# A recommendation tower on one core: TensorE's order of turns, products and gram units in each tile of 128 rows

## Chip, cores and metric

The kernel runs on 1 core of one Trainium2 chip. The metric is the device time of one execution in microseconds (us); lower is better.

## What is computed

For each of 2048 rows the reference takes one row of 128 numbers from each of 27 tables, forms all 351 dot products of two different ones of these 27 vectors, and sends vectors, dot products and 16 further numbers through three layers.

```python
e = jnp.stack([tbl_0[ids[:, 0]], ..., tbl_26[ids[:, 26]]], axis=1)      # (2048, 27, 128)
gram = jnp.einsum('bfd,bgd->bfg', e, e)                                 # (2048, 27, 27)
h = concatenate([e.reshape(B, -1), gram[:, triu_i, triu_j], dense_ctx], axis=1)   # 3823 columns
h = jnp.maximum(h @ W_top1 + b_top1, 0.0)                               # 3823 x 512
h = jnp.maximum(h @ W_top2 + b_top2, 0.0)                               # 512 x 256
y = h @ W_top3                                                          # 256 x 1
```

## The kernel before

The batch is cut into 16 tiles (t = 0 to 15) of 128 rows. The 27 features of a tile lie in seven groups (g = 0 to 6) of four, the last of three. Each engine has its whole program written out by hand in its own order, and the engines meet only at semaphores. Tiles 0 to 14 have one loop body each on TensorE, ScalarE and VectorE; tile 15 has an order of its own, which the change leaves as it is.

What happens to a tile, by engine:

- GpSimd gathers the rows of the tables into `emb`, one indirect DMA for each feature (L242). There is one `emb` for all tiles: before it gathers group g of tile t+1 it waits on `s_pe_t` until TensorE has turned group g of tile t (L236). It works strictly in the order of the groups.
- TensorE turns a group (`turn_group`, L263: four transposes at L269 into one of two banks of `ps_t`, then one increment of `s_pe_t`). It waits for the gather of the group (`s_gather`) and for the group two back to have left its bank (`s_emb_lo`, L267).
- ScalarE copies the turned group from `ps_t` into the high part of `emb_x` (`split_group`, L528, the copy is L534), VectorE subtracts to get the low part (L645) and raises `s_emb_lo`. Turn, copy and subtraction together make the group ready.
- TensorE multiplies each feature by its weights (`multiply`, L289: three matmuls of 128x512, L298 to L300, into `ps_acc`, called "one product" here). The first product of a group waits for `s_emb_lo`.
- The gram stage: 16 units of two matmuls (`gram_unit`, L308, the matmul is L323) into three banks of `ps_gram`. Unit 0 waits until the last group is ready (L310). Unit n waits until unit n-3 has been copied out. ScalarE copies out the even units (L582, four copies each), VectorE the odd ones (L666).
- VectorE turns, adds and packs the dot products of tile t-1 into `cols` during the products of tile t (L680 to L706).
- The columns' product of tile t-1 is part of tile t: TensorE turns `cols` (`turn_columns`, L359, L352), ScalarE copies it (`take_columns`, L546), TensorE adds it to the sum of tile t-1 (`multiply_columns`, L376, L356) and raises `s_acc`. ScalarE applies the relu (`relu_h1`, L561), TensorE turns h1 (`turn_h1`, L390, L393), ScalarE copies it (`take_h1`, L567), and after the gram stage TensorE makes layer 2 (`layer_2`, L397, L400). VectorE ends it (`layer_3`).

ScalarE takes its instructions in order: a copy that waits holds all that stand behind it. So in tile t the order on ScalarE is: groups 0 to 3, `take_columns`, group 4, `relu_h1`, group 5, `take_h1`, group 6, then the even units.

TensorE's order in a tile 1 to 14 before: products of group 0, turn of group 2, products of group 1, turn 3, products of group 2, `turn_columns`, turn 4, `multiply_columns`, products of group 3, turn 5, `turn_h1`, two products, turn 6, two products (`BEFORE_UNIT[0]`), gram units 0 to 15 with one or two products ahead of some, and with the turns of groups 0 and 1 of the next tile behind units 8 and 14, then `layer_2` and the products that are left.

Of the kernel before, what the change touches and what calls it, by code (L numbers as in the profile page):

```python
# [5 lines left out]
def dlrm_tower_kernel(nc, dense_ctx, ids, tables, w_top1, b_top1, w_top2, b_top2, w_top3, out):  # L6
# [7 lines left out]
    BATCH, NF = ids.shape  # L14
# [10 lines left out]
    GF = 4  # L25
    GROUPS = [list(range(f, min(f + GF, NF))) for f in range(0, NF, GF)]
    NG = len(GROUPS)
# [18 lines left out]
    UNITS = Q // QB  # L46
# [8 lines left out]
    with ctx:  # L55
# [84 lines left out]
        def emb_part(part, f):  # L140
            return emb_x[:, part, :, f]
# [4 lines left out]
        def turned_bank(n, g):  # L146
            return ps_t[:, n % 2, 0:GF * P].rearrange("p (b f) -> p b f", f=GF)[:, :, 0:len(GROUPS[g])]
# [114 lines left out]
        def _(pe):  # L262
            def turn_group(t, g):  # L263
                n = NG * t + g
                pe.wait_ge(s_gather[g], (t + 1) * 16 * len(GROUPS[g]))
                if n >= 2:
                    pe.wait_ge(s_emb_lo, n - 1)  # L267
                for i, f in enumerate(GROUPS[g]):
                    last = pe.transpose(turned_bank(n, g)[:, :, i], emb[:, f * D:(f + 1) * D],  # L269
                                        ident[:, :])  # L270
                last.then_inc(s_pe_t, 1)
# [17 lines left out]
            def multiply(t, f):  # L289
                g = f // GF  # L290
                if f == 0 and t >= 2:
                    pe.wait_ge(s_h1, t - 1)
                if f == GROUPS[g][0]:
                    pe.wait_ge(s_emb_lo, NG * t + g + 1)
                    if t == 0:
                        pe.wait_ge(s_w_lo, GROUPS[g][-1] + 1)
                acc = ps_acc[:, t % 2, :]
                pe.matmul(acc, emb_part(0, f), w_hi[:, f, :], start=(f == 0), stop=False)  # L298
                pe.matmul(acc, emb_part(0, f), w_lo[:, f, :], start=False, stop=False)  # L299
                last = pe.matmul(acc, emb_part(1, f), w_hi[:, f, :], start=False, stop=False)  # L300
                if f == GROUPS[g][-1]:
                    last.then_inc(s_emb_mm, 1)

            def multiply_group(t, g):
                for f in GROUPS[g]:
                    multiply(t, f)

            def gram_unit(t, k):  # L308
                if k == 0:
                    pe.wait_ge(s_emb_lo, NG * t + NG)  # L310
                    if t == 0:
                        pe.wait_ge(s_pads, 1)
                n = UNITS * t + k
                if n >= BANKS:

                    m = n - BANKS
                    if m % 2 == 0:
                        pe.wait_ge(s_act_raw, m // 2 + 1)
                    else:
                        pe.wait_ge(s_dve_raw, m // 2 + 1)  # L320
                for i in range(QB):
                    q = k * QB + i
                    last = pe.matmul(  # L323
                        ps_gram[:, n % BANKS, i * NJ * XW:(i + 1) * NJ * XW],
                        gram_weights(q), gram_stream(q), start=True, stop=True)
                last.then_inc(s_gram, 1)
# [32 lines left out]
            def turn_columns(t):  # L359
                pe.wait_ge(s_cols, t + 1)  # L360
                if t > 0:
                    pe.wait_ge(s_h2, t)
                if t == 0:
                    pe.wait_ge(s_ones, 2)
                for n in range(NCC):
                    last = turn_chunk(n, ps_late[:, n * P:(n + 1) * P])
                last.then_inc(s_cols_t, 1)
# [8 lines left out]
            def multiply_columns(t):  # L376
                pe.wait_ge(s_cols_out, t + 1)
                if t == 0:
                    pe.wait_ge(s_w_late, 64)
                for n in range(NCC):  # L380
                    last = multiply_chunk(t, n)
                last.then_inc(s_acc, 1)
# [7 lines left out]
            def turn_h1(t):  # L390
                pe.wait_ge(s_h1, t + 1)
                for k in range(K2):
                    last = pe.transpose(ps_late[:, k * P:(k + 1) * P], h1[:, k * P:(k + 1) * P],  # L393
                                        ident[:, :])
                last.then_inc(s_h1_t, 1)
# [42 lines left out]

            BEFORE_UNIT = [2, 0, 0, 2, 0, 0, 1, 0, 0, 1, 0, 0, 1, 0, 0, 0]
            assert len(BEFORE_UNIT) == UNITS and sum(BEFORE_UNIT) <= NF - 4 * GF

            pe.wait_ge(s_ident, 1)
            turn_group(0, 0)
            turn_group(0, 1)
            for t in range(TILES - 1):
                multiply_group(t, 0)  # L450
                turn_group(t, 2)
                multiply_group(t, 1)
                turn_group(t, 3)
                multiply_group(t, 2)
                if t > 0:
                    turn_columns(t - 1)
                turn_group(t, 4)
                if t > 0:
                    multiply_columns(t - 1)
                multiply_group(t, 3)  # L460
                turn_group(t, 5)
                if t > 0:
                    turn_h1(t - 1)
                f = 4 * GF
                for _ in range(GF if t == 0 else 2):
                    multiply(t, f)
                    f += 1
                turn_group(t, 6)
                for k in range(UNITS):
                    for _ in range(min(BEFORE_UNIT[k], NF - f)):  # L470
                        multiply(t, f)
                        f += 1
                    gram_unit(t, k)
                    if k in (8, 14):
                        turn_group(t + 1, (k - 8) // 6)
                if t > 0:
                    layer_2(t - 1)
                while f < NF:
                    multiply(t, f)
                    f += 1  # L480

            t = TILES - 1
            todo = list(range(NF))

            def multiply_next(count):
                for _ in range(count):
                    multiply(t, todo.pop(0))

            turn_group(t, 2)
            multiply_next(6)
            turn_group(t, 3)
            multiply_next(6)
# [27 lines left out]
        def _(act):  # L522
# [83 lines left out]
            for t in range(TILES - 1):  # L606
                for g in range(NG):
                    if t == 0:
                        for c in GROUPS[g]:
                            split_weights(c)  # L610
                    split_group(t, g)
                    if t > 0 and g == 3:
                        take_columns(t - 1)
                    if t > 0 and g == 4:
                        relu_h1(t - 1)
                    if t > 0 and g == 5:
                        take_h1(t - 1)
                for k in range(0, UNITS, 2):
                    take_blocks(t, k)
            t = TILES - 1  # L620
# [178 lines left out]
```

## Time and profile before

| what | value |
|---|---|
| median of 3 runs | 712.8 us (710.17 to 718.01) |
| the profiled execution, its own time | 709.83 us |
| span of the profiled execution, first to last instruction | 708.0 us |
| mean granted TensorE clock | 0.908 of full speed |
| TensorE matmuls busy | 574.9 us, 81% of the span |
| GpSimd busy | 416.2 us, 59% |
| VectorE busy | 347.6 us, 49% |
| ScalarE busy | 232.3 us, 33% |

Rows of the profile name an engine (PE TensorE's matmuls, PEld its weight loads, DVE VectorE, ACT ScalarE, POOL GpSimd), a source line (L298), what is written <- what is read, and for a stretch of instructions their number (x6). Times are microseconds from the start of the span. A number in square brackets is how long the engine stood idle just ahead of that instruction, and what released it; "remote" and "issue" say that the profile found no instruction that did. A row of stretches has from:to, its length, the busy time and count of PE, PEld, DVE, ACT and POOL, the granted TensorE clock as a share of full speed, the share of the DMA engines and GB/s.

### The profile page before, as it was taken

The numbers are of one execution on the slowest core, as the hardware profiler recorded it, in microseconds if no ns is written. First come the engines' busy times: TensorE is split into PE (matmuls) and PEld (weight loads), VectorE is DVE, ScalarE is ACT, GpSimd is POOL, SyncE is SP. The second block draws the span as 40 slices with busy tenths as digits, with TensorE's granted clock in tenths as the row PEclk, the third lists the DMA queues.
The fourth block names the chain that finished last, engine by engine and source line by source line (L and its number), as shares of the span: only waits on it lengthen the run. The fifth ranks groups of instructions, "written<-read, shape, count | busy, mean of one in ns | idle before, by whom it ended". The sixth has DMA issues, their size and how long they took to land.

```text
span 708.0 us, 7882 instructions
## 1 busy us (share of the span) xinstructions
PE 574.9 (81%) x2578; PEld 504.6 (71%) x2578; DVE 347.6 (49%) x1140; ACT 232.3 (33%) x703; POOL 416.2 (59%) x450
## 2 busy tenths in 40 slices
PE   2606688989889898959959896897968979698898
PEld 1505577868778787948848795786857868697786
DVE  4305462819264563808337281554707355372755
ACT  4204423324251513315232331514315161323441
POOL 6775565666666565665746667365664666556001
PEclk9956899989989998989989899799987999989999
DMA  6613411111111111111111111011110111111000
GB/s 211 217 52 110 131 45 44 46 46 44 45 45 50 41 49 41 48 45 39 47 29 50 44 42 52 27 49 42 46 52 26 49 41 49 42 41 46 12 1 1
DMA packets 19581, 37.84 MB, mean 53 GB/s; under 512 B 7780, under 2 KB 8804, under 8 KB 19540
## 3 DMA queue, kind: packets, MB, share of 16 engines
q0 software_dynamic: 13824, 28.34, 15.1%
q1 hardware_dynamic: 5716, 8.99, 4.0%
q8 instruction: 21, 0.34, 0.2%
q14 instruction: 20, 0.16, 0.1%
HBM read 37.30 MB, written 0.01 MB: 53 GB/s over the span
## 4 chain that ended last, share of the span: by engine, by line
PE 59%; another core or an unknown queue 20%; DVE 8%; issue 6%; ACT 5%; DMA 1%; SPq 0%; ACTq 0%; DVEq 0%
PE ps_acc L298 12%; PE ps_acc L299 11%; PE ps_acc L300 11%; PE ps_gram L323 10%; DVE g_buf L666 6%; PE ps_acc L356 6%; PE ps_t L269 5%; PE ps_gram L400 3%; ACT g_buf L582 2%; DVE emb_x L645 1%; DMA g_buf<-in_W_top 1%; ACT emb_x L534 1%; ACT h_t L571 1%; PE ps_gram L352 1%
## 5 line engine op out<-in xcount | busy, mean ns | idle before, releaser
L242 POOL DMA_INDIRECT emb<-in_tbl,idx x405 | 385.8, 953 | 233.4 <-issue 109.4
L298 PE MATMUL ps_acc<-w_hi,emb_x 128*128 128x512 f32 x432 | 211.1, 489 | 28.7 <-DVE emb_x L645 26.6
L645 DVE TENSOR_TENSOR emb_x<-ps_t,emb_x 128x512 fp32r<-128x512 f32 (+1 forms) x111 | 73.9, 667 | 249.6 <-ACT emb_x L534 165.2
L299 PE MATMUL ps_acc<-w_lo,emb_x 128*128 128x512 f32 x432 | 182.7, 423 | 0.0
L300 PE MATMUL ps_acc<-w_hi,emb_x 128*128 128x512 f32 x432 | 181.0, 419 | 0.0
L666 DVE COPY g_buf<-ps_gram 32x112 f32<-32x112 f32 x480 | 129.8, 270 | 93.6 <-PE ps_gram L323 63.1
L323 PE MATMUL ps_gram<-emb_x 128*128 128x224 f32 x480 | 99.5, 335 | 79.2 <-DVE emb_x L645 41.2
L298 PEld LDWEIGHTS ps_acc<-w_hi,emb_x 128*128 128x128 f32 x432 | 131.9, 305 | 35.3 <-DVE emb_x L645 28.0
L323 PEld LDWEIGHTS ps_gram<-emb_x 128*128 128x128 f32 x480 | 83.4, 231 | 102.0 <-DVE emb_x L645 45.1
L582 ACT ACTIVATE g_buf<-ps_gram 32x112 f32<-32x112 f32 x480 | 122.2, 255 | 99.0 <-PE ps_gram L323 64.8
L534 ACT ACTIVATE emb_x<-ps_t 128x512 fp32r<-128x512 f32 (+1 forms) x111 | 63.1, 583 | 272.7 <-PE ps_t L269 137.4
L299 PEld LDWEIGHTS ps_acc<-w_lo,emb_x 128*128 128x128 f32 x432 | 134.4, 311 | 3.9
L300 PEld LDWEIGHTS ps_acc<-w_hi,emb_x 128*128 128x128 f32 x432 | 132.6, 307 | 4.2
L269 PE MATMUL ps_t<-ident,emb 128*128 128x128 f32 x429 | 68.7, 284 | 17.5 <-DMA emb<-in_tbl,idx_first 17.1
L269 PEld LDWEIGHTS ps_t<-ident,emb 128*128 128x128 f32 x429 | 53.8, 146 | 24.6 <-issue 13.2
L680 DVE STREAM_TRANSPOSE g_buf<-g_buf 128x1792 f32<-128x1792 f32 x16 | 59.2, 3697 | 0.1
L356 PE MATMUL ps_acc<-w_cols,cols_t 128*128 128x512 f32 (+1 forms) x96 | 45.5, 609 | 4.7 <-issue 3.8
L702 DVE TENSOR_TENSOR cols<-gram,g_buf 128x26 f32<-128x26 f32 (+25 forms) x406 | 39.0, 174 | 0.0
L356 PEld LDWEIGHTS ps_acc<-w_cols,cols_t 128*128 128x128 f32 (+1 forms) x96 | 17.0, 190 | 23.3 <-issue 20.8
L242 POOL DMA_INDIRECT emb<-in_tbl,idx_first x27 | 26.9, 996 | 9.2 <-issue 7.9
L400 PE MATMUL ps_gram<-w,h_t 128*128 128x256 f32 x112 | 27.0, 385 | 0.0
L400 PEld LDWEIGHTS ps_gram<-w,h_t 128*128 128x128 f32 x112 | 20.7, 195 | 2.3
(61 smaller groups left out, 163.2 us busy)
## 6 DMA issues: line engine op xcount, KB each, us to landing
g_buf<-in_W_top SPq DMA_DIRECT2D x27, 256.0 KB
emb<-in_tbl,idx POOLq DMA_INDIRECT x405
w_cols<-in_W_top SPq DMA_DIRECT2D x1, 512.0 KB
w<-in_W_top SPq DMA_DIRECT2D x1, 512.0 KB
emb<-in_tbl,idx_first POOLq DMA_INDIRECT x27
w_cols<-in_W_top SPq DMA_DIRECT2D x1, 222.0 KB
idx<-in_ids SPq DMA_DIRECT2D x1, 216.0 KB, 4.9
ctx_rows<-in_dense_ctx SPq DMA_DIRECT2D x4, 32.0 KB
```

What stands on the lines that cost most here:

```text
L242: pool.indirect_dma_start(out=emb[:, f * D:(f + 1) * D], out_offset=None, in_=tables[f], in_offset=bass.IndirectOffsetOnAxis(ap=rows, axis ...
L269: last = pe.transpose(turned_bank(n, g)[:, :, i], emb[:, f * D:(f + 1) * D], ident[:, :])
L298: pe.matmul(acc, emb_part(0, f), w_hi[:, f, :], start=(f == 0), stop=False)
L299: pe.matmul(acc, emb_part(0, f), w_lo[:, f, :], start=False, stop=False)
L300: last = pe.matmul(acc, emb_part(1, f), w_hi[:, f, :], start=False, stop=False)
L323: last = pe.matmul(ps_gram[:, n % BANKS, i * NJ * XW:(i + 1) * NJ * XW], gram_weights(q), gram_stream(q), start=True, stop=True)
L356: return pe.matmul(ps_acc[:, t % 2, :], cols_t[0:k, n * P:(n + 1) * P], w_cols[0:k, n, :], start=False, stop=(n == NCC - 1))
L400: last = pe.matmul(ps_late[:, 0:H2], h1_t[:, k * P:(k + 1) * P], w_2[:, k, :], start=(k == 0), stop=(k == K2 - 1))
L534: act.activation(group_part(0, g), turned_bank(n, g), ACT.Copy).then_inc(s_emb_hi, 1)
L582: last = act.activation(target, source, ACT.Copy)
L645: dve.tensor_tensor(group_part(1, g), turned_bank(n, g), group_part(0, g).bitcast(fp32), ALU.subtract).then_inc(s_emb_lo, 1)
L666: last = dve.tensor_copy(target, source)
```

## The change

In tiles 1 to 14 TensorE turns group 2 ahead of the products of group 0, group 3 ahead of those of group 1, group 4 ahead of those of group 2. Then come `turn_columns`, turn 5, two products, turn 6, `multiply_columns`, four products, `turn_h1`, and the gram stage. `BEFORE_UNIT[0]` goes from 2 to 0, so 18 of 27 products stand ahead of unit 0 where 20 stood, and four are left behind layer 2 where two were. ScalarE's order becomes groups 0 to 4, `take_columns`, groups 5 and 6, `relu_h1`, `take_h1`, the even units. Tile 0 keeps its order up to turn 6 and loses the two products ahead of unit 0; tile 15 is as before.

```diff
--- before.py
+++ after.py
@@ -438,55 +438,52 @@
 
 
 
-
-
-            BEFORE_UNIT = [2, 0, 0, 2, 0, 0, 1, 0, 0, 1, 0, 0, 1, 0, 0, 0]
-            assert len(BEFORE_UNIT) == UNITS and sum(BEFORE_UNIT) <= NF - 4 * GF
+            BEFORE_UNIT = [0, 0, 0, 2, 0, 0, 1, 0, 0, 1, 0, 0, 1, 0, 0, 0]
+            assert len(BEFORE_UNIT) == UNITS
+
+            def multiply_next(count):
+                for _ in range(min(count, len(todo))):
+                    multiply(t, todo.pop(0))
 
             pe.wait_ge(s_ident, 1)
             turn_group(0, 0)
             turn_group(0, 1)
             for t in range(TILES - 1):
-                multiply_group(t, 0)
-                turn_group(t, 2)
-                multiply_group(t, 1)
-                turn_group(t, 3)
-                multiply_group(t, 2)
-                if t > 0:
+                todo = list(range(NF))
+                if t == 0:
+
+                    for g in range(2, NG):
+                        multiply_next(GF)
+                        turn_group(t, g)
+                else:
+
+
+                    turn_group(t, 2)
+                    multiply_next(GF)
+                    turn_group(t, 3)
+                    multiply_next(GF)
+                    turn_group(t, 4)
+                    multiply_next(GF)
                     turn_columns(t - 1)
-                turn_group(t, 4)
-                if t > 0:
+                    turn_group(t, 5)
+                    multiply_next(2)
+                    turn_group(t, 6)
                     multiply_columns(t - 1)
-                multiply_group(t, 3)
-                turn_group(t, 5)
-                if t > 0:
+                    multiply_next(4)
                     turn_h1(t - 1)
-                f = 4 * GF
-                for _ in range(GF if t == 0 else 2):
-                    multiply(t, f)
-                    f += 1
-                turn_group(t, 6)
                 for k in range(UNITS):
-                    for _ in range(min(BEFORE_UNIT[k], NF - f)):
-                        multiply(t, f)
-                        f += 1
+                    multiply_next(BEFORE_UNIT[k])
                     gram_unit(t, k)
                     if k in (8, 14):
                         turn_group(t + 1, (k - 8) // 6)
                 if t > 0:
                     layer_2(t - 1)
-                while f < NF:
-                    multiply(t, f)
-                    f += 1
+                multiply_next(len(todo))
 
 
 
             t = TILES - 1
             todo = list(range(NF))
-
-            def multiply_next(count):
-                for _ in range(count):
-                    multiply(t, todo.pop(0))
 
             turn_group(t, 2)
             multiply_next(6)
@@ -609,11 +606,10 @@
                         for c in GROUPS[g]:
                             split_weights(c)
                     split_group(t, g)
-                    if t > 0 and g == 3:
+                    if t > 0 and g == 4:
                         take_columns(t - 1)
-                    if t > 0 and g == 4:
+                    if t > 0 and g == 6:
                         relu_h1(t - 1)
-                    if t > 0 and g == 5:
                         take_h1(t - 1)
                 for k in range(0, UNITS, 2):
                     take_blocks(t, k)
```

## Rows read from the trace of the kernel before

**Rows 1.** Busy by stretch: 13 stretches, each from one layer 2 to the next.

```profile
246.60:286.30 39.70, 35.65 (x163) 31.68 (x162) 20.88 (x71) 13.71 (x45) 25.84 (x28) 0.91 0.18 46
286.30:329.50 43.20, 34.38 (x163) 30.58 (x162) 20.74 (x71) 13.80 (x44) 25.80 (x28) 0.92 0.16 42
329.50:373.20 43.70, 34.98 (x163) 30.99 (x162) 20.79 (x72) 13.79 (x44) 25.90 (x28) 0.92 0.16 41
...
412.60:458.20 45.60, 36.37 (x162) 31.83 (x162) 20.75 (x71) 13.78 (x44) 26.68 (x28) 0.89 0.15 40
...
497.50:543.30 45.80, 37.31 (x162) 32.61 (x161) 20.81 (x72) 13.84 (x44) 26.48 (x28) 0.85 0.15 40
...
sum 535.70, PE 461.55 PEld 408.44 DVE 270.18 ACT 177.54 POOL 330.83; mean PE 35.50 PEld 31.42 DVE 20.78 ACT 13.66 POOL 25.45
```

**Rows 2.** Timeline of TensorE in the stretch of 246.6 to 286.3.

```profile
260.73 2.85 PE L356 MATMUL ps_acc<-w_cols,cols_t 128*128 128x512 f32 x6 [0.49 <-issue]
...
266.21 0.60 PE L269 MATMUL ps_t<-ident,emb 128*128 128x128 f32 x4
266.65 0.60 PE L393 MATMUL ps_gram<-ident,h 128*128 128x128 f32 x4
...
268.59 0.49 PE L269 MATMUL ps_t<-ident,emb 128*128 128x128 f32 x3
...
273.66 1.62 PE L323 MATMUL ps_gram<-emb_x 128*128 128x224 f32 x6 [3.06 <-DVE emb_x L645]
```

**Rows 3.** Timeline of ScalarE in the same stretch.

```profile
264.42 0.60 ACT L565 ACTIVATE h<-ps_acc 128x512 f32<-128x512 f32 x1 [2.27 <-PE ps_acc L356]
271.55 0.60 ACT L534 ACTIVATE emb_x<-ps_t 128x512 fp32r<-128x512 f32 x1 [6.53 <-remote]
272.04 0.59 ACT L571 ACTIVATE h_t<-ps_gram 128x512 f32<-128x512 f32 x1
...
278.74 1.05 ACT L582 ACTIVATE g_buf<-ps_gram 32x112 f32<-32x112 f32 x4 [2.13 <-PE ps_gram L323]
```

**Rows 4.** Timeline of GpSimd in the same stretch.

```profile
254.46 0.97 POOL L242 DMA_INDIRECT emb<-in_tbl,idx  x1 [2.10 <-PE ps_t L269]
255.74 0.94 POOL L242 DMA_INDIRECT emb<-in_tbl,idx  x1 [0.30 <-issue]
...
271.79 0.94 POOL L242 DMA_INDIRECT emb<-in_tbl,idx  x1 [2.62 <-remote]
```

**Rows 5.** Chain of waits in the same stretch: start, length, what.

```profile
249.79 0.24 PE ps_acc L298
...
264.46 7.06 another core or an unknown queue
...
275.74 0.43 PE ps_acc L299
```

**Rows 6.** Timeline in the last tile, where no gather is left.

```profile
676.21 0.60 PE L269 MATMUL ps_t<-ident,emb 128*128 128x128 f32 x4
676.85 0.60 ACT L534 ACTIVATE emb_x<-ps_t 128x512 fp32r<-128x512 f32 x1 [4.24 <-PE ps_t L269]
```

**Rows 7.** Timeline of TensorE, gram units in the stretch of 412.6 to 458.2.

```profile
442.36 1.62 PE L323 MATMUL ps_gram<-emb_x 128*128 128x224 f32 x6 [6.10 <-issue]
...
448.68 0.48 PE L323 MATMUL ps_gram<-emb_x 128*128 128x224 f32 x2 [2.11 <-ACT g_buf L582]
```

**Rows 8.** Timeline of ScalarE in that stretch.

```profile
429.26 0.60 ACT L565 ACTIVATE h<-ps_acc 128x512 f32<-128x512 f32 x1 [2.45 <-PE ps_acc L356]
...
434.22 0.60 ACT L571 ACTIVATE h_t<-ps_gram 128x512 f32<-128x512 f32 x1 [1.11 <-PE ps_gram L393]
441.23 0.49 ACT L534 ACTIVATE emb_x<-ps_t 128x384 fp32r<-128x384 f32 x1 [6.41 <-issue]
```

**Rows 9.** Timeline of GpSimd: two gathers behind a wait, no other such between them.

```profile
420.05 1.49 POOL L242 DMA_INDIRECT emb<-in_tbl,idx  x1 [2.08 <-PE ps_t L269]
...
453.83 0.94 POOL L242 DMA_INDIRECT emb<-in_tbl,idx  x1 [8.94 <-PE ps_t L269]
```

## Prediction, made before the changed kernel was run

> **What bounds the kernel now.** I read the stretches by tile first, then one tile on each engine, then the chain of waits, then the tiles that are longer than the rest. The 13 stretches from one layer 2 to the next take 535.7 us, 41.2 each, and TensorE is busy for 35.5 of each [rows 1]. So TensorE is the bound, with 5.7 us a tile in which it stands. The stretches are not alike: four (43.2, 43.7, 45.6, 45.8, sum 178.3) have a mean of 44.6, the other nine (535.7 - 178.3) / 9 = 39.7 [rows 1].
>
> In the 39.7 us tile the wait is in one place. Unit 0 of the gram stage starts at 273.66 after 3.06 us idle, released by VectorE's subtraction of the last group [rows 2]. That group had been turned from 268.59. The turn ahead of it, of group 5, has its last transpose end at 266.81, and ScalarE's copy of it starts only at 271.55, after 6.53 us of idle [rows 2, 3]. The chain calls this "another core or an unknown queue", 7.06 us [rows 5]. GpSimd, which waits for the same increment, goes on at 271.79 after 2.62 us [rows 4]: two engines agree that the news of a finished turn came some 4.7 us late. I call this the **late release**. In the last tile, where no gather runs, the same handoff takes 676.85 - 676.81 = 0.04 us [rows 6]. So the lateness belongs to stretches in which gathers run, and I have no more of its cause than that: in this tile it ended 2.4 us after GpSimd had run dry (271.55 against 271.79 - 2.62 = 269.17) [rows 3, 4], in a tile below it ended in the middle of a run [rows 8, 9].
>
> The long tiles are those in which the release of turn 5 was not late and the one of turn 6 was. In the tile of 412.6, ScalarE takes h1's turn at 434.22 and gets group 6 at 441.23, 6.41 us idle [rows 8]; unit 0 starts after 6.10 us of idle and unit 3 waits another 2.11 [rows 7]. GpSimd ran without a pause from 420.05 for 19 gathers there, until 453.83 - 8.94 = 444.89 [rows 9], where in the shorter tile it ran 12, stood, and went on [rows 4].
>
> **Part 1: turns earlier, their cover.** Nothing is added or removed on any engine: 27 products, seven turns, 16 units, the columns, h1's turn and layer 2 stay, and no wait is new. Turn 6 moves from two products ahead of the products' end to the other side of the columns' product. Between turn 6 and unit 0 stood four matmul groups of 0.24 us x 3 x 2 products = 1.4 us and now stand the columns' product, 6 x 0.43 = 2.6 us (its row has 2.85 with the last one's tail), four products, 12 x 0.24 = 2.9, and h1's turn, 0.44 (266.65 to the next product) [rows 2, 5]: 5.9 us. The chain after the turn, once released, needs a copy on ScalarE of 0.6, VectorE's subtraction and back: 273.66 - 271.55 = 2.1 us for both groups and h1's copy [rows 2, 3]. A release up to 3.8 us late is therefore hidden at unit 0. Turns 2 to 4 gain one group of products each; their buffers and inputs are free by then, since the turned groups leave within two groups of products, so I cost them at nothing. The cover is VectorE's dot-product work, and if it were gone the price would be a part of one group's 2.9 us.
>
> **Part 2: the columns' product.** Before, TensorE stood 0.49 us for `cols` to be copied [rows 2]; now turn 5, two products and turn 6 lie between, 2.2 us. That stall goes in the tiles that have it: bound 0 to 13 x 0.49 = 6.4 us, I take 2.
>
> **Part 3: h1's chain, which is what is late next.** ScalarE now has `relu_h1`, `take_h1` and then unit 0's copies in line, and h1's turn is the last thing ahead of unit 0. The relu is covered by four products, 2.9 us, against 0.84 (acc's last matmul ends at 263.58, ScalarE starts at 264.42) + 0.6 = 1.4 [rows 2, 3]. `take_h1` is not: it waits for h1's turn, whose release was as late as the others (ended 267.25, at ScalarE by 271.6 to 272.04: 4.3) [rows 2, 3]. Units 0 to 2 can run, then the two products of `BEFORE_UNIT[3]`, then unit 3 waits for unit 0's copy. Let R be the release of h1's turn. Before, unit 0 starts at R + 2.1 and units 0 to 2 take 3 x 0.43 = 1.3 (their row's spacing, 1.62 with the tail, [rows 2]), so they end at R + 3.4 with 20 products done. After, unit 3 may start at R' + 0.6 (copy of h1) + 1.05 (four copies of unit 0) = R' + 1.7, with 20 products and units 0 to 2 done too [rows 3]. R' lies later in TensorE's program by two products and turn 6, 1.44 + 0.33 = 1.8 us. So the same point is reached at R + 3.5 against R + 3.4. **With an equal lateness of 4.3 us the good tiles gain nothing: the stall moves from unit 0 to unit 3.** If this lateness is shorter than the cover behind it (three units and two products, 1.3 + 1.4 = 2.7 us, less the 1.7 of copies: 1.0), the stall goes wholly.
>
> Here one rule of the Trainium skill speaks otherwise. The page "TensorE: Matmul & The Clock Gate", section "The cost: per-tile semaphore tail", gives the tail of an increment as about 25 + 4.7 + 26.3 = 56 ns for one tile and one increment, and says matmuls finish in order. The last tile agrees (0.04 us, [rows 6]), the handoff of 4.7 us with gathers running does not. By the rule h1's turn would cost no stall, and the sum would be that of the second rival below.
>
> **Part 4: the long tiles.** Their extra time is 4 x (44.6 - 39.7) = 19.6 us, all from a late release of turn 6 (or turn 5) right ahead of unit 0 [rows 1, 7, 8]. With turn 6 on the other side of the columns' product it has 3.8 us of slack and stands earlier in GpSimd's run, where releases were less late (columns' product: 0.84). I take all of it, bound 0 to 19.6.
>
> **Part 5: the rest.** Tile 0 loses two products as cover ahead of unit 0: 0 to 1.4 us, I take 1. VectorE's and ScalarE's orders change only in ScalarE's three moves; behind `take_columns` now stands turn 5's copy, behind `relu_h1` stand h1's copy and the even units. Turn 2 comes four products behind layer 2 where it came six, since four are left there now. GpSimd gets its releases for groups 5 and 6 some 5 us earlier; it is paced at 0.94 + 0.30 = 1.25 us a gather, 27 of them 33.7 us a tile [rows 4], so it allows no tile shorter than 33.7.
>
> **Clock.** In the 39.7 us tile products take 0.24 us for most of the tile and 0.43 behind the stall at unit 0 [rows 5], the two levels of 2.4 and 1.2 GHz; the granted clock over the tile is 0.91 [rows 1]. Nine products' matmuls ran there at the slow pace, 9 x 0.19 = 1.7 us. An equal stall at unit 3 costs the same; a vanished one gives it back.
>
> **Sum.** 709.8 (the profiled execution) - 19.6 - 2 + 1 = 689.2 us. The profiled execution lies 3 us under the median of 712.8, which I add back in part, for the long tiles vary from run to run: **690 us**.
>
> **Rivals.**
>
> 1. **The run of gathers stays unbroken, and every tile becomes like the two longest (slower).** GpSimd paused in the good tiles because turn 5's release was late, and the late releases ended in that pause; gram units then fell into a fresh run, where releases are prompt. With turns 5 and 6 released early, GpSimd runs 19 gathers, 25 us, and h1's turn and units 0 to 5 fall into its second half, where 434.22 to 441.23 and the next wait at unit 3 lie [rows 7 to 9]. Then `take_h1` is 6 us late and the odd units' copies later again, which the change gives no more cover than three units. It decides if h1's release is more than 1.5 to 2 us later than the 4.3 of Part 3. A tile of 45.7 us in all 14 would be 14 x (45.7 - 41.2) = 63 us more; turn 6 has cover now, so about half: 2.3 us a tile, 32 us, **742 us**. For it: both unbroken runs of the trace are in the longest tiles. Against: two tiles only, and in both it was turn 6 that waited.
> 2. **The late release is hidden wholly.** If h1's turn is released within 1 us, the 3.0 of idle and the 1.7 of slow clock go in the nine good tiles and in the long ones as well: 14 x 4.7 = 66 us below the 690, 624; GpSimd's 33.7 a tile and the copies of the units leave less, so about **640 us**. The rule of the Trainium skill in Part 3, from "TensorE: Matmul & The Clock Gate", gives this result. For it: the last tile. Against: h1's release was late in the tiles looked at, by 4.3 in the good one.
> 3. **Nothing changes within 1% (706 to 720).** The long tiles' gain is eaten by a stall at unit 3 that is 1.4 us longer than the one at unit 0 was: **710 us**.
>
> **Chances.** Forecast 0.35, rival 1 0.30, rival 2 0.15, rival 3 0.20. A measurement of this kernel tells about 1%, 7 us. Faster by over 1% is the forecast and rival 2, 0.50; within 1% 0.20; slower 0.30. The range takes the forecast and rival 3 whole, rival 1 up to its price and rival 2 down to 652, three quarters of the way from 690 to its 640; what is left out is the far half of rivals 1 and 2, some 0.2. The forecast's own range, with Part 4's bound, is 680 to 712.
>
> **What the profile after would show.** Right: TensorE's idle before unit 0 near 0, a new idle of about 3 us before unit 3 released by ScalarE's L582 behind L571; no stretch above 42 us; L356 without idle. Rival 1: GpSimd without pause through 19 gathers, L571 6 us or more behind L393, and gram updates late. Rival 2: PEclk near 1.0, stretches of 35 to 37 us, GpSimd nearly without waits. The prediction is wrong if acc's release, too, moves into the late part of the run: then TensorE stands before h1's turn, a place where it never stood.

## The result

The changed kernel takes 775.2 us (median of 4 runs, 769.8 to 777.3) against 714.1 for the kernel before (4 runs, 710.2 to 718.0): a ratio of 1.084, 95% interval 1.076 to 1.092. It is 8.4% slower where 3% faster was forecast. Of the cases in the prediction rival 1, the slower one, comes nearest, and the loss is nearly twice the 32 us that I had put on it (742). Some executions of each kernel run over 1.5% longer than its fastest one; ratios and their intervals here leave those out.

The same stretches from one layer 2 to the next, after (tiles 3 to 15 again, columns as in [rows 1]):

```profile
134.10:180.20 46.10, 34.12 (x163) 30.71 (x162) 20.67 (x72) 13.69 (x44) 25.55 (x28) 0.89 0.15 39
...
271.80:316.50 44.70, 36.38 (x163) 30.84 (x162) 20.66 (x72) 13.67 (x44) 25.39 (x28) 0.92 0.16 40
...
497.30:541.10 43.80, 34.89 (x163) 31.04 (x162) 20.52 (x71) 13.81 (x44) 25.17 (x27) 0.88 0.15 40
...
sum 587.80, PE 466.60 PEld 406.30 DVE 269.40 ACT 178.15 POOL 329.25; mean PE 35.89 PEld 31.25 DVE 20.72 ACT 13.70 POOL 25.33
```

The 13 stretches take 587.8 us where they took 535.7 [rows 1]: 45.2 a tile instead of 41.2. TensorE is busy for 35.9 of each instead of 35.5, which is 5 of the 52 us; the other 47 are waits. The shortest stretch, 43.8, is as long as the first long ones of before. Nothing is left of the 39.7 us tiles.

Who waited, on TensorE, in the changed kernel over the same tiles (in total, times, longest; us):

```profile
PE ps_gram L393 <- issue: 39.0, 8, 10.5
PE ps_gram L393 <- ACT h L562: 34.5, 4, 11.1
PE ps_acc L356 <- ACT cols_t L548: 22.6, 6, 3.9
PE ps_acc L356 <- issue: 7.8, 3, 3.1
PE ps_gram L323 <- DVE g_buf L662: 7.5, 17, 0.5
PE ps_gram L323 <- ACT g_buf L579: 6.5, 13, 1.8
```

and in the kernel before:

```profile
PE ps_gram L323 <- DVE emb_x L645: 39.0, 11, 7.7
PE ps_gram L323 <- issue: 12.3, 3, 6.1
...
PE ps_acc L356 <- issue: 3.6, 9, 0.8
PE ps_acc L356 <- ACT cols_t L551: 0.8, 4, 0.2
```

The wait ahead of unit 0 (39.0 for the last group's subtraction, and the two long ones of the 12.3) is gone, as meant. In its place stand 73.5 us ahead of h1's turn (L393), where before there was nothing, and 30.4 ahead of the columns' product (L356), where there were 4.4.

One tile on the engines shows the chain. TensorE:

```profile
283.08 0.60 PE L269 MATMUL ps_t<-ident,emb 128*128 128x128 f32 x4
...
286.81 0.60 PE L269 MATMUL ps_t<-ident,emb 128*128 128x128 f32 x4
...
288.77 0.49 PE L269 MATMUL ps_t<-ident,emb 128*128 128x128 f32 x3
...
292.98 4.36 PE L356 MATMUL ps_acc<-w_cols,cols_t 128*128 128x512 f32 x6 [3.73 <-ACT cols_t L548]
...
303.77 0.66 PE L393 MATMUL ps_gram<-ident,h 128*128 128x128 f32 x4 [3.44 <-issue]
```

ScalarE, same tile:

```profile
283.71 0.60 ACT L531 ACTIVATE emb_x<-ps_t 128x512 fp32r<-128x512 f32 x1 [2.79 <-issue]
292.38 0.38 ACT L547 ACTIVATE cols_t<-ps_gram 128x256 f32<-128x256 f32 x1 [8.07 <-remote]
...
295.22 0.60 ACT L531 ACTIVATE emb_x<-ps_t 128x512 fp32r<-128x512 f32 x1 [2.29 <-remote]
300.92 0.49 ACT L531 ACTIVATE emb_x<-ps_t 128x384 fp32r<-128x384 f32 x1 [5.10 <-remote]
303.12 0.60 ACT L562 ACTIVATE h<-ps_acc 128x512 f32<-128x512 f32 x1 [1.71 <-remote]
...
306.79 0.60 ACT L568 ACTIVATE h_t<-ps_gram 128x512 f32<-128x512 f32 x1 [3.08 <-remote]
```

GpSimd, same tile:

```profile
279.53 0.94 POOL L242 DMA_INDIRECT emb<-in_tbl,idx  x1 [2.19 <-remote]
...
295.46 0.94 POOL L242 DMA_INDIRECT emb<-in_tbl,idx  x1 [1.27 <-remote]
...
301.15 0.94 POOL L242 DMA_INDIRECT emb<-in_tbl,idx  x1 [1.02 <-remote]
...
312.42 0.94 POOL L242 DMA_INDIRECT emb<-in_tbl,idx  x1 [7.83 <-PE ps_t L269]
```

Turn 4 ends at 283.68 and ScalarE takes it at 283.71: prompt, and early in a run of gathers that began at 279.53. Turn 5 ends at 287.41 and is taken at 295.22 (7.8 us late), turn 6 ends at 289.26 and is taken at 300.92 (11.7 late), the columns' product ends at 297.34 and relu takes acc at 303.12 (5.8 late). GpSimd was idle from 295.46 - 1.27 = 294.19 and again from 300.13: turn 5 came out 1.0 us after the first break, turn 6 0.8 us after the second. The other two came out while GpSimd gathered on: the columns' turn (taken at 292.38, with the run from 279.53 still going) and acc (taken at 303.12, with gathers at 302.40 and 303.65). Each of the late releases is a link of TensorE's own next step now: the columns' copy holds L356 for 3.73, acc holds L393 for 3.44 (in other tiles up to 11.1).

The same reading over the 13 tiles of each trace. The first three rows give how long after the modelled end of TensorE's work ScalarE took it; a run is a series of gathers with no idle time of 0.9 us or more between them. ScalarE works in order, so where a copy ahead was late the figure holds that too (h1 before in nine tiles, acc after in two).

| in 13 tiles | before | after |
|---|---|---|
| turned columns | 0.04 to 0.65 us | 0.04 to 1.24 in four tiles, 3.3 to 5.6 in nine |
| acc (columns' product) | 0.04 to 1.53 us | 0.9 in one tile, 4.6 to 13.3 in twelve |
| turned h1 | 1.3 to 4.8 us | 0.04 to 2.4 us |
| GpSimd's run from group 2 on | 12 gathers in ten tiles, 16 in one, 19 in two | 12 in eight, 16 in two, 19 in three |

So the runs of gathers are hardly longer than before. In ten of the 13 tiles the run still breaks off after 12 or 16 gathers, and these tiles take 44 to 48 us all the same.

### The profile page after: what moved, and what is told of

The parts are those of the page before. It is cut to its first block, busy times and chain, and to the rows that moved or that the text cites. A ratio compares the mean times of both kernels' runs of the same rounds, so it can differ in the third digit from the quotient of the medians.

```text
span 768.0 us, 7882 instructions
## 1 busy us (share of the span) xinstructions
PE 578.0 (75%) x2578; PEld 502.0 (65%) x2578; DVE 346.7 (45%) x1140; ACT 232.9 (30%) x703; POOL 414.8 (54%) x450
## 3 DMA queue, kind: packets, MB, share of 16 engines
q0 software_dynamic: 13824, 28.34, 14.0%
## 4 chain that ended last, share of the span: by engine, by line
PE 45%; another core or an unknown queue 28%; issue 12%; DVE 8%; ACT 3%; POOL 1%; DMA 1%; ACTq 0%; DVEq 0%
PE ps_acc L298 9%; PE ps_acc L299 8%; PE ps_acc L300 8%; DVE g_buf L662 7%; PE ps_gram L323 6%; PE ps_t L269 5%; PE ps_gram L400 3%; PE ps_acc L356 3%; ACT g_buf L579 2%; POOL emb L242 1%; PE ps_gram L393 1%; DVE w_lo L634 1%; DMA emb<-in_tbl,idx_first 1%; DVE emb_x L641 0%
## 5 line engine op out<-in xcount | busy, mean ns | idle before, releaser
L299 PE MATMUL ps_acc<-w_lo,emb_x 128*128 128x512 f32 x432 | 179.9, 416 | 0.0
L298 PEld LDWEIGHTS ps_acc<-w_hi,emb_x 128*128 128x128 f32 x432 | 132.2, 306 | 35.9 <-DVE emb_x L641 26.6
L323 PE MATMUL ps_gram<-emb_x 128*128 128x224 f32 x480 | 95.6, 326 | 23.8 <-ACT g_buf L579 8.7
L323 PEld LDWEIGHTS ps_gram<-emb_x 128*128 128x128 f32 x480 | 79.0, 224 | 42.1 <-DVE g_buf L662 17.8
L356 PE MATMUL ps_acc<-w_cols,cols_t 128*128 128x512 f32 (+1 forms) x96 | 58.6, 757 | 31.9 <-ACT cols_t L548 22.6
L269 PE MATMUL ps_t<-ident,emb 128*128 128x128 f32 x429 | 67.0, 278 | 19.8 <-issue 13.3
L393 PE MATMUL ps_gram<-ident,h 128*128 128x128 f32 x60 | 14.0, 375 | 83.5 <-issue 49.0
L393 PEld LDWEIGHTS ps_gram<-ident,h 128*128 128x128 f32 x60 | 9.1, 186 | 87.8 <-issue 51.9
L356 PEld LDWEIGHTS ps_acc<-w_cols,cols_t 128*128 128x128 f32 (+1 forms) x96 | 20.2, 224 | 54.3 <-issue 29.5
L547 ACT ACTIVATE cols_t<-ps_gram 128x256 f32<-128x256 f32 x15 | 5.7, 383 | 88.7 <-remote 75.3
```

The source lines that it names most:

```text
L323: last = pe.matmul(ps_gram[:, n % BANKS, i * NJ * XW:(i + 1) * NJ * XW], gram_weights(q), gram_stream(q), start=True, stop=True)
L356: return pe.matmul(ps_acc[:, t % 2, :], cols_t[0:k, n * P:(n + 1) * P], w_cols[0:k, n, :], start=False, stop=(n == NCC - 1))
```

## The experiments

The runs fall into four sets, and the kernel before ran in each, on the same chip as the others of the set. Its median was 709.8 us in the first, 710.4 in the second, 696.2 in the third and 693.0 in the fourth, so ratios are taken within a set. No run of the changed kernel is on record beside them. Two theories were to be told from their rivals. Theory 1: TensorE's increments come late only beside the gathers. Theory 2: they pile up late in an unbroken run of gathers and come out when the run breaks off, so what costs is where a handoff falls in GpSimd's run. The rivals put the loss down to TensorE's dense stream or to the new order itself.

**1. No gathers.** In both kernels the gathers of tiles 1 to 15 are left out.

```diff
-            for t in range(TILES):
+            for t in range(1):
...
-                pe.wait_ge(s_gather[g], (t + 1) * 16 * len(GROUPS[g]))
+                pe.wait_ge(s_gather[g], 16 * len(GROUPS[g]))
```

> The kernel before, but the gathers of tiles 1 to 15 are left out (every tile turns the rows of tile 0), with the waits on them. All else stays. Theory 1 (the semaphore increments of TensorE arrive late only while gathers run): every handoff from TensorE is prompt, unit 0 of a tile waits under 1 us, a tile takes about 35 us, the run about 712 - 14 x 6 = 625 to 640 us. Rival (the lateness comes from TensorE's own dense stream of matmuls): ScalarE still gets turn 5 some 4 us late and the time stays above 695 us.

> The changed kernel with the same gathers left out. Theory 1: the order of the change is harmless by itself, no stall of more than 1 us before h1's turn, and the time is within 1.5% of the kernel before without gathers. Rival (ScalarE's new order, with both copies of h1's chain right ahead of the even units, is itself what is slow): it stays 5 to 8% slower than the kernel before without gathers.

Measured: 585.5 us for the kernel before, 578.0 for the changed one (one run each). TensorE's waits in 400 us of the kernel before without gathers, then of the changed one:

```profile
PE ps_gram L322 <- DVE g_buf L665: 10.7, 24, 0.4
PE ps_acc L355 <- ACT cols_t L550: 2.5, 12, 0.2
```

```profile
PE ps_gram L322 <- DVE g_buf L661: 9.1, 24, 0.4
```

Theory 1 stands and its rival falls: without gathers TensorE's stream is as dense as it can be, and TensorE waits 13 and 9 us of 400. I had expected 625 to 640. The tiles take 33.9 and 33.5 us, less than my 35, and the first layer 2 of these stretches comes 30 us earlier in the kernel before (at 98.1 instead of 127.7), which I hadn't counted. The order of the change does no harm by itself: it is 1.3% faster, in one run each. Its loss exists only beside the gathers.

**2. The same bytes without GpSimd.** The changed kernel with plain copies of 128 rows in place of the gathers, from SyncE.

```diff
+            for t in range(1, TILES):
+                for g in range(NG):
+                    sp.wait_ge(s_pe_t, NG * (t - 1) + g + 1)
+                    for f in GROUPS[g]:
...
+                        sp.dma_start(emb[:, f * D:(f + 1) * D], tables[f][0:P, :]).then_inc(landed, 16)
```

> The changed kernel, with the gathers of tiles 1 to 15 replaced by plain copies of the same size (the first 128 rows of each table, 128 x 512 B) issued by SyncE; same number of transfers, same bytes, same waits for TensorE's turns, but no indirect transfers and nothing on GpSimd. Theory 1a (lateness comes from GpSimd making the indirect transfers): near the time without gathers, within 2%. Theory 1b (it comes from the landing of any 27 x 128 rows of 512 B): acc is released late as in the changed kernel and the time is 740 us or more.

Measured: 585.3 us, within 1.3% of the 578.0 without gathers. 1b falls: the landing of 27 x 128 rows of 512 B does not hurt.

**3. Plain copies issued by GpSimd**, the same with `pool.dma_start`; then with a scratch tile cleared behind each copy (384, later 720 columns), so that GpSimd is as busy as with gathers.

```diff
+                        pool.dma_start(emb[:, f * D:(f + 1) * D], tables[f][0:P, :]).then_inc(landed, 16)
+                        if fills:
+                            pool.wait_ge(s_fill, fills)
+                        pool.memset(idle_cols[:, :], 0.0).then_inc(s_fill, 1)
+                        fills += 1
```

> The changed kernel with the indirect gathers of tiles 1 to 15 replaced by plain copies of the same size (first 128 rows of each table, one after the other), still issued by GpSimd. Theory 1a' (any descriptor made by GpSimd's software delays TensorE's increments): acc still comes late by more than 4 us in most tiles, 740 us or more if GpSimd takes as long per transfer. Rival (it is the indirect form alone): prompt as with SyncE's copies, 580 to 600 us.

> As the run with plain copies issued by GpSimd, but GpSimd clears 384 columns of a scratch tile behind each copy, so that a transfer takes it 1.1 to 1.3 us instead of 0.54 and it is as busy as with the gathers. If the late increments come from GpSimd being busy without a break, or from transfers in flight without a break: late again, above 700 us. If they come from the indirect form of the transfer: prompt, 575 to 610 us.

> Plain copies by GpSimd with 720 columns cleared behind each, so that a transfer takes 1.25 us or more, as long as a gather, and GpSimd runs without a pause through most of a tile. If it is the unbroken run as such: above 700 us with late increments. If it is the indirect form: increments prompt, 575 to 620 us (over 590 only if GpSimd itself becomes the bound).

Measured: 578.1, 577.2 and 577.2 us (one run each). The first left GpSimd idle half of the time and the second was faster than a gather (0.89 us from copy to copy), so only the third settles it. Its stretch of 400 us (busy PE, PEld, DVE, ACT, POOL, clock, DMA share, GB/s), and what GpSimd waited for in it:

```profile
120.00:520.00 400.00, 389.90 (x1926) 354.64 (x1925) 248.75 (x850) 162.51 (x512) 388.79 (x665) 1.00 0.19 55
```

```profile
POOL emb L247 <- PE ps_t L275: 7.6, 6, 1.6
POOL emb L247 <- issue: 2.9, 4, 0.8
```

GpSimd is busy for 389 of 400 us, a transfer every 1.17 us, and has no breaks worth the name, 7.6 us in all. TensorE is busy for 390 with the clock full. ScalarE takes acc and h1's turn 0.04 us after their end in each of twelve tiles, though GpSimd goes on for up to 93 copies without a break. So neither the unbroken run as such nor plain transfers issued by GpSimd make TensorE's increments late.

**4. The indirect form with rows in order.** The gathers stay, but all take rows 0 to 127.

```diff
-                        rows = idx_first[:, f:f + 1] if t == 0 else idx[:, t, f:f + 1]
+                        rows = idx_first[:, f:f + 1] if t == 0 else row_no[:, 0:1]
```

> The changed kernel with its indirect gathers, but of tiles 1 to 15 every gather takes rows 0 to 127 of its table by an index tile made once, instead of rows spread over the table. Same instruction, same bytes, same pace on GpSimd. If the late increments come from the indirect instruction: as the changed kernel, 760 to 785 us. If they come from reads spread over the memory: prompt, 575 to 620 us.

Measured: 775.5 us (one run), near the changed kernel's 775.2. TensorE's waits, 120 to 720 us (L397 is h1's turn there):

```profile
PE ps_gram L397 <- issue: 63.6, 7, 10.8
PE ps_gram L397 <- ACT h L566: 51.0, 6, 11.5
```

Reads spread over the tables are not the cause. With equal sizes and destinations, what is left between this run and the plain copies by GpSimd is the indirect instruction (0.94 us and more of work on GpSimd each, where a plain copy has 0.54); both send 13824 packets, 28.34 MB, through the same queue. Whether rows in order are exactly as slow as spread ones isn't told, since the kernel before took 693.0 us beside this run and 714.1 beside the changed kernel.

**5. Another break in the run of gathers, kernel before.**

```diff
-                        pool.wait_ge(s_pe_t, NG * (t - 1) + g + 1)
+                        pool.wait_ge(s_pe_t, NG * (t - 1) + (NG if g == 5 else g + 1))
```

> The kernel before with one wait changed: GpSimd's gathers of group 5 wait for turn 6 instead of turn 5, so that the run of gathers always breaks off after group 4 until both late turns are released. Nothing else moves. Theory 2 (a late increment comes out when a run of gathers breaks off): the four long tiles of 43 to 46 us become like the others, 39 to 40 us, and the time falls by about 20 us, to 688 to 698 us. Rival (lateness has nothing to do with where the run breaks; GpSimd only loses time): 712 to 730 us.

Measured: 693.7 us (4 runs) against 710.4, a ratio of 0.970, interval 0.958 to 0.983. TensorE's waits, 120 to 660 us:

```profile
PE ps_gram L323 <- DVE emb_x L645: 26.7, 10, 3.3
PE ps_acc L356 <- issue: 15.7, 12, 3.9
```

The long tiles are gone but for one of 43.5; the mean of the 13 stretches is 525.4 / 13 = 40.4. The wait ahead of unit 0 is 26.7 where it was 39.0 and most of 12.3. A wait more on GpSimd makes the kernel faster, by 1.7 to 4.2%; theory 2 gave 688 to 698.

**6. The same break in the changed kernel.**

> The changed kernel with the gathers of group 5 waiting for turn 6 instead of turn 5, as was done to the kernel before. Theory 2 (increments pile up late in a run and come out when it breaks off): turns 5 and 6 and acc come out at one break instead of at two or three, the stall before h1's turn falls from a mean of about 8 us to under 5, and a tile from 45 us to 41 or 42: 715 to 735 us. Rival (another break does nothing for a run that is already late): within 1.5% of the changed kernel, 765 to 785 us.

Measured: 718.5 us (2 runs) against 696.2, a ratio of 1.041, interval 1.022 to 1.059. The loss is 4.1% with the wait and was 8.4% without it (in another set): one wait on GpSimd undoes about half.

```profile
PE ps_gram L323 <- ACT g_buf L579: 21.8, 9, 10.3
PE ps_gram L323 <- DVE g_buf L662: 17.9, 24, 1.7
PE ps_gram L393 <- ACT h L562: 14.2, 7, 2.8
...
PE ps_gram L393 <- issue: 8.9, 2, 5.3
```

These are TensorE's waits from 120 to 680 us. The stall ahead of h1's turn, over 13 tiles, falls from 73.5 to 23.1. What rises is the wait of gram units for copies, from 14.7 (120 to 722 us) to 39.7. Its longest, 10.3 and 4.6 us, stand ahead of unit 3: the stall of Part 3 of the prediction.

**7. A longer break, up to h1's turn.**

```diff
+                    if t > 1 and g == 5:
+                        pool.wait_ge(s_h1_t, t - 1)
```

> The changed kernel with one wait more: GpSimd's gathers of group 5 wait until TensorE has turned h1. The run breaks off after 12 gathers, ahead of the end of the columns' product, and starts again behind h1's turn. Theory 2: acc and h1's turn are released within 2 us, TensorE's stall of about 10 us before h1's turn goes to under 3, and most of the loss is undone: 700 to 725 us. Rival (the order itself is at fault): the stall before h1's turn stays above 6 us and the time above 755 us.

Measured: 785.9 and 816.7 us. This missed. TensorE from h1's turn on, in one tile (L395 is h1's turn there, L325 the gram unit):

```profile
303.50 0.66 PE L395 MATMUL ps_gram<-ident,h 128*128 128x128 f32 x4 [0.50 <-ACT h L564]
...
314.70 0.84 PE L325 MATMUL ps_gram<-emb_x 128*128 128x224 f32 x4 [2.55 <-issue]
...
318.27 0.77 PE L325 MATMUL ps_gram<-emb_x 128*128 128x224 f32 x2 [2.73 <-DVE g_buf L664]
...
321.80 0.77 PE L325 MATMUL ps_gram<-emb_x 128*128 128x224 f32 x2 [1.90 <-ACT g_buf L581]
```

The stall at h1's turn did go, to 0.50 here and 4.9 in all: that half of the theory holds. GpSimd stands there until h1 is turned, and ScalarE took h1's turn 0.04 us after its end in all 13 tiles. But the gathers held back now run together with the gram stage, whose 16 units are a chain of handoffs with a cover of three units, and units wait 2.55, 2.73 and 1.90 us, 94.5 in all from 120 to 740 us. This break moved the late releases to other handoffs and didn't remove them.

**8. One part of the change at a time.** The turns two groups ahead, with columns and h1 at before's places, as they are and with the break of experiment 5; and before's order with h1's turn alone moved to just ahead of unit 0. The first as an edit to the changed kernel:

```diff
                     turn_columns(t - 1)
                     turn_group(t, 5)
-                    multiply_next(2)
-                    turn_group(t, 6)
                     multiply_columns(t - 1)
-                    multiply_next(4)
+                    multiply_next(GF)
+                    turn_group(t, 6)
                     turn_h1(t - 1)
+                    multiply_next(4)
```

> One part of the change alone: turns two groups of products ahead, but the columns' product after 12 products and h1's turn after 16 with four products between h1's turn and unit 0 (the order of ScalarE: group 4, columns, group 5, relu, group 6, copy of h1). Theory 2 (what costs is the pair of handoffs of h1's chain at the end, where nothing covers them): most of the loss goes, 700 to 730 us. Rival (what costs is that turns 5 and 6 are released early and the gathers run without a pause): it stays at 755 to 775 us.

> The turns two groups ahead with the columns' product and h1's turn at before's places, plus the same wait of group 5's gathers for turn 6. Theory 2: the loss of 5% of the turns alone goes, since turns 5 and 6 come out together; 690 to 710 us, and if the turns' new places are worth anything by themselves it is under the 694 us of the kernel before with this wait. Rival: the turns released early keep TensorE's later increments late; above 725 us.

> One part of the change alone, on the kernel before: h1's turn moves from behind turn 5 to just ahead of gram unit 0, and its copy on ScalarE behind group 6. Turns and columns stay. If what hurts is h1's chain at the end of the products with nothing to cover it: slower by 3% or more, 733 us up, with a stall before unit 3. If what hurts is only the turns released early: within 1% of before.

Measured: the turns ahead 745.6 against 709.8, a ratio of 1.053 (1.042 to 1.064), between the two expectations; with the break 701.5, 715.2, 720.8 and 722.0 against 696.2. Only the first of these four lies in the 690 to 710 that I had expected, and the other three are over 1.5% above it, so this expectation is neither met nor missed. h1's turn last: 711.6 against 710.4, 1.000 (0.994 to 1.005), no change. TensorE's waits with the turns ahead, 120 to 700 us:

```profile
PE ps_acc L356 <- ACT cols_t L548: 49.0, 8, 7.1
PE ps_acc L356 <- issue: 17.4, 5, 6.3
```

So the turns alone cost 5.3 of the 8.4%: 66.4 us of wait ahead of the columns' product, whose turned `cols` now is the release that comes late. One tile, GpSimd, TensorE and ScalarE:

```profile
228.40 0.97 POOL L242 DMA_INDIRECT emb<-in_tbl,idx  x1 [2.15 <-PE ps_t L269]
233.94 0.49 PE L352 MATMUL ps_gram<-ident,cols 128*128 128x128 f32 x3
241.32 0.39 ACT L547 ACTIVATE cols_t<-ps_gram 128x256 f32<-128x256 f32 x1 [7.97 <-remote]
```

The columns are turned 234.43 - 228.40 = 6.0 us after the run of gathers began, and taken 6.9 us late. Over 13 tiles they are turned 6.0 to 6.2 us into the run and taken 2.6 to 6.9 us late in twelve. In the kernel before they are turned 5.3 to 6.4 us into the run and never over 0.65 us late. This speaks against theory 2 as it stands: the same handoff, as far into a run, is prompt in one order and late in the other, so where it falls in the run doesn't settle it.

h1's turn last costs nothing in before's order. Its waits, 120 to 664 us:

```profile
PE ps_gram L323 <- ACT g_buf L582: 29.1, 16, 3.3
PE ps_gram L323 <- DVE emb_x L645: 17.2, 11, 2.1
```

The wait for VectorE ahead of unit 0 fell to 17.2 (from 39.0) and the wait for ScalarE's copies rose to 29.1 (from 10.0 over the same 544 us); all of TensorE's waits come to 77.9, from 75.5. So a stall moved and nothing was gained or lost, as the sum of Part 3 has it, but not for its reason. ScalarE took h1's turn within 1.2 us of its end in twelve of 13 tiles, and the waits of over 1.5 us for ScalarE's copies stand ahead of unit 9 in ten tiles, not of unit 3.

**9. A version faster than both.** Before's order, the break of experiment 5, and the columns turned two products earlier.

```diff
+                multiply(t, 2 * GF)
+                multiply(t, 2 * GF + 1)
                 if t > 0:
                     turn_columns(t - 1)
+                multiply(t, 2 * GF + 2)
+                multiply(t, 2 * GF + 3)
```

> The kernel before with the wait of group 5's gathers for turn 6, and with the columns turned two products earlier (between the second and the third product of group 2), so that TensorE's wait for their copy, 15.7 us in all in the run with that wait alone, is covered by 1.4 us a tile. If nothing else comes late: 10 to 15 us under the run with the wait alone, a ratio to before of 0.95 to 0.965. If lateness just moves to acc: the same as that run, 0.97.

Measured: 683.9 us (10 runs, 682.2 to 687.0) against 693.0 (15 runs, 687.0 to 708.2), a ratio of 0.990, interval 0.986 to 0.994. It is 1% faster than the kernel before, but the ratio missed: the kernel before itself ran at 693 here. Whether it is better than the break alone isn't told, since the two never ran in one set, and since it contains that break, the 3% of experiment 5 isn't shown to hold on this chip. The wait ahead of L356 did go, and the one ahead of unit 0 is 43.4, over 120 to 660 us (26.7 with the break alone, 39.0 in the kernel before; L648 is the subtraction there):

```profile
PE ps_gram L323 <- DVE emb_x L648: 43.4, 13, 4.2
```

## Why the prediction was wrong, point by point

**What bounds the kernel: right.** TensorE and its waits on late releases. The source of the lateness was left open and is now narrowed: it needs the indirect gathers (experiments 1 to 4). That it belongs to the gathers was in the text, and rival 1 was built on it. One reading was wrong: in the tile of 286.3 to 329.5, one of the four long ones, turn 5 too was late (ended 306.22, taken at 309.50), so "the release of turn 5 was not late" holds for three of the four.

**Part 1, turn 6's cover at unit 0: right in its place, wrong as a gain.** Unit 0 no longer waits for the last group. But of turns 2 to 4 the text says "I cost them at nothing": I asked only whether their buffers and inputs were ready. The turns alone cost 5.3% (experiment 8), and 66.4 us of wait stand ahead of the columns' product there, against 4.4. Earlier turns release GpSimd's gathers earlier, which may be the link. But the runs are hardly longer (table above), so how an earlier turn makes the columns' release late isn't shown.

**Part 2, the columns' product: wrong in sign.** I took 2 us of gain. Its wait rose from 4.4 to 30.4, since the increment of `turn_columns` came 5.4 us late in the tile shown (ended 286.98, taken at 292.38), against 2.2 us of cover; in nine of 13 tiles it was 3.3 to 5.6 us late. I had priced the move by an order in which the release was prompt.

**Part 3, h1's chain: the failed step.** "The relu is covered by four products, 2.9 us, against 0.84 [...] + 0.6 = 1.4". The 0.84 is acc's lateness in one tile of the old order, carried over to the new one. In the new order acc's release was 5.8 us late in the tile shown and 4.6 to 13.3 us in twelve of 13, so h1's turn waited up to 11.1 us at once and 73.5 in all, more than the whole loss. The columns' price in Part 2 and the zero for the earlier turns in Part 1 are the same step: a release was taken to be as late in its new place as in its old one. The prediction's last sentence names this case and gives it no chance of its own. The second half of Part 3 wasn't tested by the change: it takes h1's turn to be 4.3 us late, and ScalarE took it 0.04 to 2.4 us after its end. h1's turn moved alone (experiment 8) has the forecast outcome, no gain, for another reason.

**Part 4, the long tiles: wrong here, right with the break.** I gave the change their 19.6 us, since turn 6 would have slack. The break took all but one of them away in the kernel before (experiment 5, 16.7 us between medians). The change made every tile as long as they were, 43.8 to 47.9 us.

**Part 5 and the clock: of little weight.** The mean granted clock went from 0.908 to 0.891, and TensorE was busy for 5 us more over the 13 stretches.

**The rivals.** Rival 1 had the direction, and its unhalved price was near: the 13 stretches measured 45.2 us each, against its 45.7 for "every tile becomes like the two longest". I halved it because "turn 6 has cover now"; the late releases fell on the next handoffs instead. 45.2 - 41.2 over 14 tiles gives 56 of the 60 us between the spans. Part of that nearness is luck, for its mechanism is not what happened. It had GpSimd run through 19 gathers in every tile, which three of 13 did, and h1's copy (L571 there) 6 us or more behind h1's turn, with the stall ahead of unit 3; measured are 2.4 us at most, and the stall ahead of h1's turn. Rival 2's time, 640 or 624, is far above the 578 that the order reaches without gathers.

**What stays open.** How an indirect gather delays TensorE's increments, why one comes out at a break and another in mid run, and what decides which handoff is late, since neither the length of the run nor the place in it does by itself (experiment 8). Experiment 7 shows that I can't yet say where in a tile a break does good. A count of the gathers into a run at which lateness begins wasn't tried.

## What to carry to other kernels

When a handoff's lateness depends on what another engine is doing, it has no price of its own: a lateness read in the old order, such as the 0.84 us here, says nothing about the new one, where it was 4.6 to 13.3. Ask of each earlier release what it sets going. Here turning earlier alone made the kernel 5.3% slower, while one more wait on GpSimd made it 3% faster on one chip. Before reordering around such a stall, leave the suspected traffic out once: that run shows both whether it is the cause and what the order is worth without it.

## What the runs showed of the hardware

Beside indirect gathers on GpSimd, increments of TensorE's semaphores arrived up to 13.3 us after the modelled end of the matmul that makes them (11.7 in the tile shown), while plain copies of the same 128 x 512 B, issued by SyncE or by GpSimd at a pace of 1.17 us, left them prompt (0.04 us; 577 to 585 us against 775). Rows in order left them late as well (775.5 us). The page "TensorE: Matmul & The Clock Gate" of the Trainium skill, section "The cost: per-tile semaphore tail", has a formula for the tail of increments; worked out for one tile and one increment it is an estimate of 56 ns. That fits the runs without gathers (0.04 us), and with them the measurement decides. Without any gathers the kernel's tiles take 33.5 to 33.9 us. The order of before takes 585.5 us then, so 124 of its 709.8 us in that set go with the gathers of tiles 1 to 15.
